# Joint attention of 32 heads: bf16 pieces on 96 rows before, three-product f32r halves on 64 rows each after

## The reference: what is computed

```python
x = x + jnp.tanh(g_xattn[0]) * _L0_xattn_ref(_layernorm(x, axis=-1), ctx_1024, ...)

q = x @ Wq + bq
k = jnp.concatenate([x @ Wks + bks, context @ Wkc + bkc], axis=1)
v = jnp.concatenate([x @ Wvs + bvs, context @ Wvc + bvc], axis=1)
q = _split_heads(q, H); k = _split_heads(k, H); v = _split_heads(v, H)      # H = 16
attn = jnp.einsum('bhqd,bhkd->bhqk', q, k) / jnp.sqrt(jnp.float32(head_dim))
attn = jax.nn.softmax(attn, axis=-1)
out = jnp.einsum('bhqk,bhkd->bhqd', attn, v)
return out @ Wo + bo
```

## Time and profile before

| | us |
|---|---|
| median of three runs | 3018.72 (3017.26 to 3019.69) |
| profiled execution | 3019.72, span 3017.8 |
| load, gates, layer norm | 0 to 30.4 |
| projections | 30.4 to 94.3 |
| stacking of the first heads | 94.3 to 108.4 |
| first maxima, until the first score | 108.4 to 124.1 |
| first scores of head 0 to head 31 | 124.1 to 625.1 |
| last head | 625.1 to 640.4 |
| turn and projection | 640.4 to 674.4 |
| all other stages | 674.4 to 3017.8 |

### The profile page before, as it was taken

How to read it: one execution, slowest core, us unless ns; L and a number is a source line. 1 busy time by engine, 2 the same in 40 slices (tenths; PEclk the granted TensorE clock), 3 DMA queues, 4 the chain that set the end, 5 groups by cost and what they waited for, 6 DMA issues and landing times. The chain is left out here.

```text
span 3017.8 us, 43014 instructions
## 1 busy us (share of the span) xinstructions
PE 2415.8 (80%) x15716; PEld 1650.5 (55%) x15716; DVE 1999.3 (66%) x4265; ACT 1255.4 (42%) x2974; POOL 937.4 (31%) x867
## 2 busy tenths in 40 slices
PE   6799999987997899759999776888888987950254
PEld 3233333336886566548888444777666776840122
DVE  4588888824766555457776346775657675579898
ACT  4266666642443544323333112646325564320121
POOL 2000000001554433225554002554335453413343
PEclk9799999996998999869999677899898998975566
DMA  1111111101001000110000001000100000010000
GB/s 71 23 27 27 30 27 27 30 19 47 1 1 58 1 1 1 41 68 1 1 1 4 22 1 47 1 1 12 68 1 1 2 1 32 1 42 0 0 1 28
DMA packets 15681, 57.90 MB, mean 19 GB/s; under 512 B 7408, under 2 KB 7408, under 8 KB 13552
## 3 DMA queue, kind: packets, MB, share of 16 engines
q1 hardware_dynamic: 15472, 55.15, 5.5%
HBM read 39.37 MB, written 2.10 MB: 14 GB/s over the span
## 5 line engine op out<-in xcount | busy, mean ns | idle before, releaser
L2298 ACT ACTIVATE probs<-psum 128x512 f32<-128x512 f32 (+1 forms) x640 | 346.7, 593 | 195.9 <-PE psum L2242 195.0
L2313 DVE TENSOR_REDUCE max_parts<-psum 128x1 f32<-128x512 f32 x512 | 328.6, 684 | 63.4 <-PE psum L2215 59.6
L152 PE MATMUL psum<-x_upper,weights_upper 128*128 128x512 f32 (+2 forms) x624 | 252.8, 405 | 26.6 <-POOL weights_rest L164 17.6
L152 PE MATMUL psum<-x_rest,weights_upper 128*128 128x512 f32 (+2 forms) x624 | 249.8, 400 | 0.0
L152 PE MATMUL psum<-x_upper,weights_rest 128*128 128x512 f32 (+2 forms) x624 | 247.1, 396 | 0.0
L152 PE MATMUL psum<-weights_upper,hidden_upper 128*128 128x256 f32 (+2 forms) x768 | 242.4, 316 | 1.8 <-DVE x_tok L311 1.7
L164 POOL TENSOR_TENSOR weights_rest<-L1f,weights_upper 128x256 fp32r<-128x256 f32 x216 | 181.4, 866 | 183.6 <-ACT weights_upper L269 183.6
L152 PE MATMUL psum<-weights_upper,hidden_rest 128*128 128x256 f32 (+2 forms) x768 | 217.2, 283 | 0.0
L152 PE MATMUL psum<-weights_rest,hidden_upper 128*128 128x256 f32 (+2 forms) x768 | 217.1, 283 | 0.0
L2253 PE MATMUL psum<-probs,v_tok 128*17 128x256 f32 (+1 forms) x2560 | 201.1, 385 | 0.4 <-ACT probs L2298 0.4
L2242 PE MATMUL psum<-q_stack,k_stack 98*128 98x512 bf16 (+1 forms) x640 | 198.3, 387 | 0.5
(11 more groups left out here) (432 smaller groups left out, 6065.4 us busy)
## 6 DMA issues: line engine op xcount, KB each, us to landing
L1f<-in_L1f SPq DMA_DIRECT2D x1, 7936.0 KB, 21.6
k_stack<-k_parts SPq DMA_DIRECT2D x192, 36.8 KB, 2.0
q_stack<-q_parts SPq DMA_DIRECT2D x192, 32.0 KB, 2.0
L0f<-in_L0f SPq DMA_DIRECT2D x1, 4760.0 KB, 14.4
L2f<-in_L2f SPq DMA_DIRECT2D x2, 2268.0 KB, 8.5
L1x<-in_L1x SPq DMA_DIRECT2D x1, 4226.0 KB, 13.2
L2a<-in_L2a SPq DMA_DIRECT2D x2, 2048.0 KB, 11.4
L3f<-in_L3f SPq DMA_DIRECT2D x1, 3072.0 KB, 10.2
```

The lines of the kernel that those rows point to most:

```text
L152: ins = pe.matmul(out, lhsT(a).bitcast(F32R), rhs(b).bitcast(F32R), start=start and n == 0, stop=stop and n == len(PASSES) - 1, skip_group ...
L2298: act.activation(pb[0:m, s % NPB, hf * 512:(hf + 1) * 512], net.ps[0:m, STB + hf, :], ACT.Exp, scale=HD ** -0.5).then_inc(exp_done, 1)
L2313: v.tensor_reduce(mx3[:, u % 2, q, k:k + 1], net.ps[:, XB + (2 * n + k) % 3, :], AX.X, ALU.max).then_inc(x_taken, 1)
```

## The change

**Stacks.** q and k are kept as an upper and a rest part in f32 instead of three bf16 pieces. Three pairings (`Q_PARTS`, `K_PARTS`) of 16 rows make 48 rows, and two rows of the maximum make 50. Queries 0 to 511 lie on partitions 0 to 49, queries 512 to 1023 on 64 to 113, and the k stack is there twice. There are still 12 DMAs a unit; the k ones carry 4712 bytes a row instead of 2356. The maximum needs four row copies instead of two.

**Loop.** A unit has five steps of two key tiles. One PSUM bank pair per key tile holds both halves, and one ACT instruction takes 1024 columns. Maximum products come in pairs, one for each half, ten pairs a unit, into a ring of three banks. The ring also carries the turned maximum and the turned output. The value products are issued in two groups of five key tiles: tiles 0 to 4 at step 3, tiles 5 to 9 at step 0 of the next unit. `probs` has ten slots. ACT, not DVE, copies the output (behind its fourth exponential) and takes the turned one (behind its eighth). Division by the sum is made once per batch element, on POOL or in the last block.

**Around it.** `layer_norm` leaves out its turning, and the projection block turns x itself, splits x, context and weights into upper and rest, and projects with `three`; DVE adds the value bias. SP stacks the first three heads within that block. The last block turns, splits and projects with `three`. `L0x` is loaded after the gates, `wo` and `bo` in a pack of their own, and `ctok` ahead of the last cross stage.

```diff
-    Q_PARTS, K_PARTS = [0, 0, 0, 1, 1, 2], [0, 1, 2, 0, 1, 0]
+    Q_PARTS, K_PARTS = [0, 0, 1], [0, 1, 0]
     ROWS = HD * len(Q_PARTS)
+    HALF = 64
...
+            for r, (i, j) in enumerate(zip(Q_PARTS, K_PARTS)):
+                for e in range(2):
+                    lo = HALF * e + r * HD
+                    sp.dma_start(qs[lo:lo + HD, s, :], qp[i][r0:r0 + HD, c, b, e * 512:(e + 1) * 512])\
+                        .then_inc(stacked[s], 16)
+                    sp.dma_start(ks[lo:lo + HD, s, :], kp[j][r0:r0 + HD, c, b, :]).then_inc(stacked[s], 16)
...
+            w = Weights(net, ctx, "L0x")
+            w_out.load()
+            xn = o_raw[:].rearrange("p t h d -> p (t h d)")[:, 0:T * D].rearrange("p (t d) -> p t d", d=D)
+            layer_norm(net, x, None, keep=xn)
...
+            @block.sync
+            def _(sp):
+                sp.wait_ge(ones_in, 3)
+                sp.wait_ge(taken, 5)
+                for u in range(NST):
+                    stack(sp, u)
...
+                for b in range(B):
+                    turn_x(b)
+                    for n in range(PER):
+                        project(b * PER + n)
+                    for k in range(NK):
+                        values(b, k)
...
-            NPB = 4
+            NPB, STEPS, AHEAD, GROUP = 10, NK // 2, 4, NK // 2
+            ST, RING, NR, PVB = 0, 4, 3, 7
...
+                    n = u * NPAIR + NPAIR + AHEAD + 2 * k
+                    here = [divmod(m, NPAIR) for m in (n, n + 1) if m < NU * NPAIR]
+                    at_step[u, k] = here
+                    for v_, i in here:
+                        ring += [("max", v_, i, e) for e in range(2)]
+                    if k == 2 and u > 0:
+                        ring.append(("out", u - 1))
+                    if k == 3 and u + 1 < NU:
+                        ring.append(("top", u + 1))
...
             @block.sync
             def _(sp):
                 for u in range(NU):
                     s = u % NST
+                    n = place["top", u]
+                    sp.wait_ge(reduced, n + 1 - outs_before[n])
                     for r, part in enumerate((hi, lo)):
+                        for e in range(2):
+                            row = HALF * e + ROWS + r
+                            sp.dma_start(qs[row:row + 1, s, :], part[4 * e:4 * e + 4, u % 2, :]).then_inc(rows_in[s], 16)
+                    if u >= 1 and u + 2 < NU:
+                        sp.wait_ge(st_done, 2 * NK * u)
+                        stack(sp, u + 2)
...
+                def enter(item):
+                    n = place[item] - NR
+                    if n >= 0:
+                        if ring[n][0] == "out":
+                            pe.wait_ge(out_taken, outs_before[n] + 1)
+                        else:
+                            pe.wait_ge(reduced, n + 1 - outs_before[n])
...
+                    for e in range(2):
+                        enter(("max", u, i, e))
+                    if kind == "self":
+                        for e in range(2):
+                            r = slice(HALF * e, HALF * e + ROWS)
+                            pe.matmul(bank(("max", u, i, e)), qs[r, s, a * P:(a + 1) * P].bitcast(F32R),
+                                      ks[r, s, k * 512:(k + 1) * 512].bitcast(F32R), start=True, stop=True)\
+                                .then_inc(made, 1)
...
+                    if n >= 2:
+                        pe.wait_ge(exp_done, n - 1)
+                    for e in range(2):
+                        r = slice(HALF * e, HALF * e + ROWS + 2)
+                        pe.matmul(net.ps[0:m, ST + 2 * (k % 2) + e, :], ks[r, s, k * P:k * P + m].bitcast(F32R),
+                                  qs[r, s, :].bitcast(F32R), start=True, stop=True).then_inc(st_done, 1)
...
+                    for k in range(STEPS):
+                        here = at_step[u, k]
+                        for v_, i in here[:1]:
+                            max_pair(v_, i)
+                        scores(u, 2 * k)
+                        scores(u, 2 * k + 1)
+                        for v_, i in here[1:]:
+                            max_pair(v_, i)
+                        if k == 2 and u > 0:
+                            turn_out(u - 1)
+                        if k == 3 and u + 1 < NU:
+                            turn_max(u + 1)
+                        if k == 0 and u > 0:
+                            for m in range(GROUP, NK):
+                                weighted(u - 1, m)
+                        if k == 3:
+                            for m in range(GROUP):
+                                weighted(u, m)
...
+                        if n >= NPB:
+                            act.wait_ge(pv_done, n - NPB + 1)
+                        act.wait_ge(st_done, 2 * (n + 1))
+                        act.activation(pb[0:m, n % NPB, :], net.ps[0:m, ST + 2 * (k % 2):ST + 2 * (k % 2) + 2, :]
+                                       .rearrange("p a n -> p (a n)"), ACT.Exp, scale=HD ** -0.5).then_inc(exp_done, 1)
+                        if k == 3 and u > 0:
+                            copy_out(u - 1)
+                        if k == 7 and u > 0:
+                            take_out(u - 1)
...
+                    for k in range(STEPS):
+                        for v_, i in at_step[u, k]:
+                            reduce_pair(v_, i)
+                            if i == NPAIR - 1:
+                                finish_max(v_)
+                        if k == 3 and u + 1 < NU:
+                            split_max(u + 1)
...
+                for g in range(G):
+                    turn_o(g)
+                    if g == 1:
+                        pe.wait_ge(wo_ready, 1)
+                    if g >= 1:
+                        project(g - 1)
+                project(G - 1)
...
+                wc = Weights(net, sub, "L3c")
```

More of the change, by code:

```diff
@@ new lines, in joint_attention, with normal, stack @@
+        qs = net.sb(attn, "q_stack", [P, NST, S // 2])
+        ks = net.sb(attn, "k_stack", [P, NST, KEYS])
+        qp = two(attn, "q_parts", [P, C, B, S])
+        kp = two(attn, "k_parts", [P, C, B, KEYS])
+        stacked = [net.sem(attn, f"stacked{k}") for k in range(NST)]
+        def normal(b, c):
+            return qp[0][:, c, b, :].rearrange("p (t h d) -> p t h d", t=QT, d=HD)
+        def stack(sp, u):
+            b, h = head(u)
+            c, r0 = h // HC, (h % HC) * HD
+            s = u % NST
+            for r, (i, j) in enumerate(zip(Q_PARTS, K_PARTS)):
[4 more added lines that the diff above has]
+                    sp.dma_start(ks[lo:lo + HD, s, :], kp[j][r0:r0 + HD, c, b, :]).then_inc(stacked[s], 16)
@@ L2207, in max_scores, with max_pair @@
+                def max_pair(u, i):
                     s = u % NST
[L2208 to L2209 removed]
+                    kind, a, k = pairs[i]
+                    if i == 0:
                         pe.wait_ge(stacked[s], 12 * 16 * (u // NST + 1))
[L2211 to L2216 removed]
@@ new lines, in turn_max, with turn_out @@
+                def turn_max(u):
+                    enter(("top", u))
+                    pe.wait_ge(max_done, u + 1)
+                    pe.transpose(bank(("top", u))[0:QT, 0:P], mx[:, u % 2, :], net.ident[:]).then_inc(made, 1)
+                def turn_out(u):
+                    enter(("out", u))
+                    pe.wait_ge(o_copied, u + 1)
+                    for i in range(2):
+                        ins = pe.transpose(bank(("out", u))[:, i * P:(i + 1) * P], ob[:, u % 2, i * P:(i + 1) * P],
+                                           net.ident[:])
+                    ins.then_inc(made, 1)
@@ L2287, in _ @@
+                for m in range(GROUP, NK):
+                    weighted(NU - 1, m)
                 turn_out(NU - 1)
@@ L2290, in _, with copy_out, take_out @@
             def _(act):
+                def copy_out(u):
+                    act.wait_ge(pv_done, (u + 1) * NK)
+                    if u >= 2:
+                        act.wait_ge(out_taken, u - 1)
+                    act.copy(ob[:, u % 2, :], net.ps[:, PVB, 0:256]).then_inc(o_copied, 1)
+                def take_out(u):
+                    b, h = head(u)
+                    act.wait_ge(made, place["out", u] + 1)
+                    src = bank(("out", u))[:, 0:2 * P].rearrange("p (i j d) -> p i j d", i=2, d=32)[:, :, :, 0:HD + 1]
+                    dst = o_raw[:, b * QT:(b + 1) * QT, h, :].rearrange("p (j i) d -> p i j d", i=2)
+                    for i in range(2):
+                        ins = act.copy(dst[:, i], src[:, i])
+                    ins.then_inc(out_taken, 1)
@@ L2345, in _, with reduce_pair @@
-                for q in range(QT):
-                    maximum(0, q)
+                v.memset(net.ps[:, PVB, :], 0.0).then_inc(ready, 1)
+                def reduce_pair(u, i):
+                    kind, a, k = pairs[i]
+                    for e in range(2):
+                        v.wait_ge(made, place["max", u, i, e] + 1)
```

(7 more changed lines are left out.)

580 lines of the change are left out of this document (311 added, 269 removed).

## The result

| | before | after |
|---|---|---|
| median, us | 3019.1 | 3118.94 (3117.69 to 3120.19, four runs) |
| ratio | | 1.0334, 95% interval 1.0321 to 1.0347 |
| span of the profiled execution | 3017.8 | 3115.7 |

The change makes the kernel 3.3% slower. It was forecast at 1.2% slower, and the time lies 9 us above the range.

The account below looks back on a forecast made before the run. PE, busy 98% of the loop, was taken to bound the kernel before the change. 3019.7 + 81.5 (loop) - 33.2 (ahead) - 11.5 (behind) = 3056.5, less 1.0 for profiled run against median: 3055.5 us, range 2995 to 3110.

Parts of the forecast that it names:

- Halves side by side, and one exponential for 1024 columns: In the loop: a pair of 512 columns costs 0.24 us instead of 0.44, an exponential of 1024 columns 1.05.
- Ahead of the loop: Projections and stacking before the loop: first maximum product starts at 75.2 instead of 108.4, -33.2 us.
- Behind it: Turning and projecting after the loop: 22.5 us instead of 34.0, -11.5 us.
- The chain at full clock, 17.4: In the loop: waits between PE, ACT, DVE and SP make a head 17.4 us at full clock, 1.2 more than before.
- E7: A head's eighth exponential; the output copy behind it frees the bank for step 3's second pair, a link of 3.1 us.
- The clock, 1.6: In the loop: PE at 1.2 GHz in the first value group of most heads, adding 1.6 us a head.
- First maxima and last head: The loop's two ends: 17.8 us from first maximum product to first score, 14.6 us for the last head.
- The sum: The whole loop: 24.5 + 31 heads at 19.0 us gives 613.5 us instead of 532.0, +81.5.
- Both value groups at 1.2 GHz: Rival for the loop: 2.2 us more a head, 21.2 us a head, 3124 us; chance 0.11.
- The clock stays full: Rival for the loop: 17.4 us a head, loop +31.9 us, 3006 us in all; chance 0.19.
- DVE is the bound: Rival for the loop: PE always answers in time, 14.0 us a head, loop 458.5, 2900 us; chance 0.08.
- p: Time of one head in the loop: forecast 19.0 us, with 18.2 to 20.2 as its own range.

Follow-up runs that it names:

- the fastest version: The changed kernel with output taken behind the sixth exponential, value products two key tiles a step, and two of four row copies issued by ACT: 2953.5 us.
- Two edits that brought 22 and 8 us alone: On the changed kernel: output taken behind the sixth exponential instead of the eighth, 3097.0 us; value products issued two key tiles per step, 3111.2 us.
- the version with both edits: The changed kernel with the output taken behind the sixth exponential instead of the eighth and value products issued two key tiles per step: 2997.7 us.
- one wait was removed: The changed kernel with ACT taking the turned output behind its sixth exponential instead of its eighth, nothing else: 3097.0 us.

## Why the prediction was wrong

The forecast for what stands ahead of the loop and behind it came out, the first partly by luck. In the loop the mechanism was right, a chain of waits and a clock that falls in every head, and its size was not: a head takes 20.4 us instead of 19.0. Two terms of that sum were too small, the chain at full clock (17.4 forecast, 18.4 measured) and what the clock adds (1.6 forecast, 2.1 measured), and so were the loop's two ends. By the steps of the prediction:

- *Halves side by side, and one exponential for 1024 columns.* Right: two key tiles' scores in 0.63, exponentials 0.92 apart where 1.05 was taken.
- *Ahead of the loop.* Forecast 75.2 for the first maximum product, measured 74.8, with two errors that cancel: the stage starts at 27.1 instead of 25.4, and from there it is 47.7 to that product instead of 49.8. Also the terms listed for the stage (25.7, 14.4, 8, 4 and 1.5) add up to 53.6 and not to the 49 that was used, so that this came out is partly luck. *Behind it:* 22.7 for 22.5. *All the rest:* +1.1 for nothing.
- *The chain at full clock, 17.4.* This is the first mis-sized term: 18.4. The places were right. The rows bring the first score at 6.0 (forecast 6.35, rounded to 6.4), as the wait at 392.48 shows, and the stack is there at 14.2, as forecast. The pair behind E7 takes 3.24 for 3.1 at 2.4 GHz. Too short was what lies between. From the first score to the pair behind the second value group 2.9 were forecast and 3.7 measured, because PE waits for DVE ahead of the pair in front of that group (322.52, 0.38 us idle) and the group itself takes 2.4. From there to the first pair of step 3 it was 4.95 forecast and 5.3 to 5.4 measured: pair after pair is 1.37 and 1.34, not 1.26, since PE starts 0.15 behind a reduction, not 0.05. That is +0.8, +0.4 and +0.1, less 0.3 for the rows: the 1.0 a head, 31 us in the loop. The 1.26 was put together from parts, and it could have been seen to be too short: DVE's two reductions alone take 1.29. With three banks PE's answer is nearly hidden behind the second of them. From 319.00 DVE takes 5.33 us for four pairs, 1.33 each, so PE's answer adds only 0.04 or 0.05.
- *The clock, 1.6.* The second mis-sized term: 20.5 less 18.4, 2.1 a head (0.5 more than forecast, 15 us in the loop). Its first part came as forecast: with the first value group at 1.2 GHz the first score stands at 7.6 instead of 6.05, and 1.5 were forecast. But the clock falls before that group, not in it. In most heads the last context pair, the first pair of step 3 and the pair behind E7 are already slow, and that is the other 0.5: the links that average 1.33, 1.59 and 3.45 are 1.09, 1.46 and 3.24 in the heads in which the clock falls only behind the first pair of step 3, like the one shown. The sign "granted clock about 0.8" was right (0.77 with PE busy 75%, between the two stretches of the earlier trace rows), "heads 19 apart" was not.
- *First maxima and last head.* Forecast 17.8 and 14.6, measured 22.9 and 18.5: 9 us together. Both were worked out at full clock, but the clock gives way here too. In the first stretch it is 0.58, and a pair takes 1.64 instead of 1.35:

```profile
76.04 0.50 PE L2314 MATMUL psum<-k_stack,q_stack 48*128 48x512 f32 x2 [0.77 <-DVE max_parts L2446]
...
80.38 0.79 PE L2314 MATMUL psum<-k_stack,q_stack 48*128 48x512 f32 x2 [0.84 <-DVE max_parts L2446]
```

  Also, in PE's order four pairs of head 1 stand ahead of the first score, and they take longer than the 4.0 us that were put down for the rows. In the last head ACT stands 3.84 us behind a value group at 1.2 GHz, where one of 2.2 was put in:

```profile
739.02 4.47 PE L2358 MATMUL psum<-probs,v_tok 128*17 128x256 f32 x40
...
744.31 1.92 ACT L2414 ACTIVATE probs<-psum 128x1024 f32<-128x1024 f32 x2 [3.84 <-PE psum L2348]
```

- *The sum.* In the loop 613.5 was forecast and 673.7 measured: 60 us. Of these 31 are the chain, 15 the clock in it, 9 the two ends. Of the other 5, 3 are two heads of 22.1 and 22.2, in which the clock fell once more; the rest is that the first head and the one ahead of the last were 6.6 us shorter than the others, and not 7.9.
- *The rivals.* "Both value groups at 1.2 GHz" gave 3124 and comes nearest in time, but its mechanism is not what happened: the second group lasts 2.4 to 2.5 us in all heads but two. "The clock stays full" (3006) fell twice: the clock did not stay, and with it held the time is 3069, since its chain was short as well. "DVE is the bound", p = 14.0, is what the fastest version comes to (14.7), and it needed three edits. The range was too narrow upwards because the chain, the clock and the two ends all erred on the same side: p was let go up to 20.2 and the ends by 5 us, and measured were 20.4 and 9.
- *The page.* The Trainium skill (TensorE: Matmul & The Clock Gate, "HAM oscillation — how this bites in real kernels") blames long idle gaps, by which p would have stayed at 17.4. Here PE is never idle for more than 1.9 us in the loop, and the clock falls in every head. The same page has a second case that I left out ("A second HAM failure mode: psum-queue depth-cycling"), a kernel in which PE idles often for short times while it cycles through PSUM banks. This loop is of that kind, and the trace agrees: it has waits of 0.4 to 1.9 us on a ring of three banks, and the clock goes between its two levels.

## What to carry to other kernels

Two edits that brought 22 and 8 us alone brought 121 together: in a loop that loses PE's clock, the clock can take back what a removed wait brings, so test such edits together, or with the clock held by idle products in the gaps. Count these products against the gaps first: too many of them made two versions slower (3284 us for 3119, 3042 for 2998). A ring of hand-overs (PE to DVE to PE) is best priced from a measured round, and never below what one engine in it works alone: 1.26 us was put down for a link in which DVE alone works 1.29. A link on another queue counts only if it ends last: two row copies on another queue were worth nothing in the changed kernel and 44 us in the version with both edits, some 28 of them at full clock.

## What the runs showed of the hardware

- More work on PE made the kernel faster. With 14 idle products of some 0.21 us a head, five of them in the longest gap, the granted clock of the loop rose from 0.77 to 0.99, and 3118.9 us became 3069.3.
- The clock of the changed kernel fell at least once in every head, although no wait of PE in the loop was longer than 1.9 us; the others have 0.4 to 0.85. In the fastest version, with pieces of value products between the pairs and without the long wait, it was 0.98.
- The pattern repeats: three lengths of heads in turn in the changed kernel, four (17.5, 19.1, 20.3, 21.7) when one wait was removed.
- The k copies grew from 36.8 to 73.6 KB and land in 2.4 instead of 2.0 us, not the 1 us more that was allowed for:

```profile
k_stack<-k_parts_upper SPq DMA_DIRECT2D x128, 73.6 KB, 2.4
```
